# Attention over 4096 tokens on one core: TensorE's order goes by two key blocks, and it sums six key blocks of a chunk instead of five

## What is computed

```python
qkv = jnp.einsum('bnc,ce->bne', x, W_qkv)      # N = 4096 tokens, C = 128
q, k, v = jnp.split(qkv, 3, axis=-1)           # 4 heads of 32
q = l2norm_axis1(q)                            # over the tokens
k = l2norm_axis1(k)
sim = jnp.einsum('bihd,bjhd->bhij', q, k) * 10.0
attn = jax.nn.softmax(sim, axis=-1)
out = jnp.einsum('bhij,bjhd->bhid', attn, v)
```

## Time and profile before

| | us |
|---|---|
| runs of the kernel | 5823.16, 5830.10, 5831.83; median 5830.1 |
| profiled execution | 5824.59 |
| its span | 5822.9 |
| TensorE busy | 4673.1 (80%) |
| VectorE busy | 5061.3 (87%) |
| ScalarE busy | 3766.6 (65%) |
| GpSimd busy | 1666.2 (29%) |
| granted TensorE clock, mean | 0.944 |

### The profile page before, as it was taken

One profiled execution on the slowest core, in us unless ns is written; L12 is line 12 of the kernel. 1 busy time (PEld: TensorE's weight loads), 2 busy tenths in 40 slices (PEclk: granted clock), 3 DMA queues, 4 the chain that ended last, 5 costly groups with the idle time before them and its releaser, 6 DMA issues. The chain is left out here.

```text
span 5822.9 us, 99803 instructions
## 1 busy us (share of the span) xinstructions
PE 4673.1 (80%) x33816; PEld 1945.2 (33%) x33880; DVE 5061.3 (87%) x6502; ACT 3766.6 (65%) x4929; POOL 1666.2 (29%) x1274
## 2 busy tenths in 40 slices
PE   5677779998766777999876677799987667779997
PEld 2222433333322243333432224333343222433334
DVE  6799769998789977999868996799986899679998
ACT  3666459993466646999346663689934666369992
POOL 1488600000048860000005885000000588500000
PEclk9899989999889998999988999899998899989998
DMA  1000020000000002000000000200000000020000
GB/s 39 0 1 0 15 63 9 9 5 23 23 0 1 0 15 63 9 9 5 22 23 0 1 0 15 63 9 9 5 22 23 0 1 0 15 63 9 9 5 15
DMA packets 41642, 87.27 MB, mean 15 GB/s; under 512 B 11672, under 2 KB 27872, under 8 KB 38112
## 3 DMA queue, kind: packets, MB, share of 16 engines
q1 hardware_dynamic: 41184, 81.11, 5.2%
HBM read 26.55 MB, written 8.39 MB: 6 GB/s over the span
## 5 line engine op out<-in xcount | busy, mean ns | idle before, releaser
L1303 ACT ACTIVATE arena<-ps 128x1024 f32<-128x1024 f32 x2048 | 1915.2, 1035 | 194.4 <-PE ps L1266 177.6
L1332 DVE TENSOR_TENSOR arena<-arena 128x1024 f32<-128x1024 f32 x1664 | 1901.4, 1216 | 32.8 <-ACT arena L1303 32.3
L941 DVE TENSOR_TENSOR_SCAN arena<-ps,hlast,arena 128x512 f32<-128x512 f32 x1024 | 1259.1, 1265 | 5.2 <-DVE arena L923 3.2
L901 POOL TENSOR_TENSOR arena<-arena 128x1024 f32<-128x1024 f32 x512 | 1205.9, 2355 | 25.0 <-issue 1.8
L1266 PE MATMUL ps<-arena 128*32 128x512 f16 x16384 | 1095.0, 383 | 123.8 <-issue 62.3
L1249 PE MATMUL ps<-arena 128*32 128x512 f32 x8192 | 1070.0, 600 | 8.0 <-ACT arena L1303 4.3
L870 ACT ACTIVATE ps<-arena,amat 128x512 f32<-128x512 f32 x1024 | 691.9, 688 | 504.9 <-DVE arena L941 504.2
L838 PE MATMUL ps<-arena,ident 128*128 128x512 f32 x2048 | 980.8, 602 | 7.7 <-POOL arena L901 7.7
L1266 PEld LDWEIGHTS ps<-arena 128*32 128x32 f16 x16384 | 466.8, 97 | 980.2 <-issue 655.6
L1646 POOL MEMSET arena<- 128x1024 f32 x4 | 3.8, 956 | 2639.6 <-POOLq L101 2639.6
L923 DVE TENSOR_TENSOR arena<-arena,ps 128x1024 f32<-128x1024 f32 x512 | 610.8, 1193 | 53.1 <-remote 30.7
(11 more groups left out here) (246 smaller groups left out, 4401.5 us busy)
## 6 DMA issues: line engine op xcount, KB each, us to landing
arena<-x SPq DMA_DIRECT2D x32, 512.0 KB, 5.5
arena<-arena SPq DMA_DIRECT2D x64, 256.0 KB, 6.0
arena<-arena SPq DMA_DIRECT2D x64, 224.0 KB, 5.7
arena<-arena SPq DMA_DIRECT2D x28, 512.0 KB, 3.6
arena<-pe SPq DMA_DIRECT2D x256, 32.0 KB, 1.8
out<-arena SPq DMA_DIRECT2D x8, 1024.0 KB, 3.9
expw<-L_ffn_expert_w SPq DMA_DIRECT2D x1, 512.0 KB
wqkv<-L_attn_W_qkv SPq DMA_DIRECT2D x1, 192.0 KB
```

Of the source, the lines that this page charges most:

```text
L901: pool.tensor_tensor(halves(g[s % 4]), halves(hb[s % 4]), cs[s % 4].unsqueeze(1).broadcast_to([128, HD, CH]), ALU.mult).then_inc(hc_s, 1)
L941: dve.tensor_tensor_scan(halves(hb[s % 4])[:, h, :], da(s, h), halves(dbx[s % 2])[:, h, :], k.hlast[:, s, h, :], ALU.mult, ALU.add).then_i ...
L1303: act.activation(probs[p % 8], k.bank(2 * group[p], 2 * CH), ACT.Exp, scale=SCALE / SPLIT ** 2).then_inc(exp_s, 1)
L1332: dve.tensor_tensor(acc[p % 2], acc[p % 2], probs[p % 8], ALU.add).then_inc(acc_s, 1)
```

## The change

The summed blocks become every fifth block from 5 on: 5, 10, 15, 20, 25 and 30, so VectorE's additions go from 54 to 52 a chunk. TensorE's order becomes: scores of an even block and of the odd one after it, then the values of two blocks: after block j (odd, from 3 on) those of j-3 and j-2. The values of the last two blocks of a chunk, 30 (with its ones) and 31, come behind block 1 of the next chunk. The boundary steps move: `finish` from behind the scores of pair 4 to pair 5, the copy of the output from exponential 2 to 4, the division from addition 5 to 6. All waits keep their form.

```diff
--- before.py
+++ after.py
@@ -1218,7 +1218,7 @@
 
     group = [p % 3 for p in range(NPAIR - 1)] + [1]
 
-    direct = [j for j in range(NJ) if j % 6 == 5]
+    direct = list(range(5, NJ, 5))
     NA = NPAIR - 2 * len(direct)
 
     def first(c):
@@ -1268,15 +1268,14 @@
                                              start=True, stop=True, tile_position=(0, 32 * t))
                     last.then_inc(s_mm, 1)
 
-                    if p == 1 and not first(c):
-                        weigh(c - 1, NJ - 1)
-                    if p == 4 and not first(c):
+                    if p == 5 and not first(c):
                         finish(c - 1, 1 - q)
-                if j in (3, 4):
-                    weigh(c, 2 * j - 6)
-                    weigh(c, 2 * j - 5)
-                if j >= 5:
-                    weigh(c, j - 1)
+                if j == 1 and not first(c):
+                    weigh(c - 1, NJ - 2)
+                    weigh(c - 1, NJ - 1)
+                if j % 2 and j > 1:
+                    weigh(c, j - 3)
+                    weigh(c, j - 2)
 
         def staged(c, i, n):
             pe.wait_ge(staged_s[i], n * 16)
@@ -1287,6 +1286,7 @@
             staged(cc * 2 + 1, 1, cc + 1)
             staged(cc * 2 + 2, 0, cc + 1)
         staged(NCH - 1, 1, NCH // 2)
+        weigh(NCH - 1, NJ - 2)
         weigh(NCH - 1, NJ - 1)
         finish(NCH - 1, (NCH - 1) % 2)
 
@@ -1301,7 +1301,7 @@
                 act.wait_ge(pv_s, c * NJ + (p // 2 + 1))
                 act.wait_ge(acc_s, summed(c, p - 8))
                 act.activation(probs[p % 8], k.bank(2 * group[p], 2 * CH), ACT.Exp, scale=SCALE / SPLIT ** 2).then_inc(exp_s, 1)
-                if p == 2 and not first(c):
+                if p == 4 and not first(c):
                     keep_output(c - 1)
 
         act.sem_inc(exp_s, 3)
@@ -1330,7 +1330,7 @@
                 else:
                     dve.wait_ge(acc_s, summed(c, p) - 2)
                     dve.tensor_tensor(acc[p % 2], acc[p % 2], probs[p % 8], ALU.add).then_inc(acc_s, 1)
-                if p == 5 and not first(c):
+                if p == 6 and not first(c):
                     divide(c - 1)
 
         dve.sem_inc(pv_s, 4)
```

## The result

The changed kernel takes 6008.5 us (median of 4 runs, 5999.0 to 6012.5) against 5830.2: ratio 1.0306, interval 1.0288 to 1.0324. Forecast was 6001 us with 5950 to 6060. The profiled execution has a span of 6010.7 us, 187.8 more than before's 5822.9.

A forecast was written before the change was run, and what follows sets the result against it. A loop of TensorE and ScalarE over three score buffers was taken as the bound. Chunks 1 to 7 gain 5.7 us each, with chunk 0 and tail 44.1 a batch, +176 on 5824.6: 6001 us, range 5950 to 6060.

The forecast's parts named there:

- The bound: In the attention, a loop between TensorE and ScalarE over three score buffers fills a chunk, 65.3 us; VectorE runs just under.
- The values' wait: TensorE's value matmuls no longer wait for their exponentials; this removes only TensorE's idle time.
- Pairing: Two value blocks after four scores: each round takes 4.04 us for exponentials needing 3.68; 16 rounds are 64.6 us a chunk.
- Sixth block: Six summed blocks lie on the loop at 0.86 us each, 5.2 a chunk; VectorE's two additions fewer gain nothing.
- Joint and tail: Between chunks, scores 63 wait one exponential more, 0.92 us; at a batch's end the tail grows by 1.4 us.
- Steps: Moved boundary steps at a chunk's start: the final sum costs 0.27 us; ScalarE's copy and VectorE's division lie in slack.
- ScalarE's idle time: Sign: idle before the exponentials, waiting for scores, near 177.6 + 176 us or a little more.
- The total: Whole kernel: 5824.6 us of the profiled execution plus 176 us gives 6001 us, 3.0% slower; chance 85%.
- A: Rival, faster: VectorE bounds the attention, so two additions fewer a chunk give 73 us, 5752 us; chance 4%.
- B: Rival: rounds without ones are free as TensorE gets ahead; +0.8 us a chunk, about 5850 us; chance 4%.
- C: Rival: TensorE's granted clock falls to 0.97 in every chunk of the attention, 64 us more, 6065 us; chance 5%.

The follow-up runs named there:

- half-width values: Changed kernel with the value matmuls of every odd block over 256 of 512 queries, the other products left out: 5814.0 us, ratio 0.9982.
- five blocks and older values: Kernel before with values of block j-2 instead of j-1 behind the scores of block j, boundary steps moved, five summed blocks: 5777.4 us, ratio 0.9918.
- fastest kernel: Kernel before with values of block j-2, moved boundary steps, six summed blocks and their ones sums between the score pairs: 5726.3 us, ratio 0.9836.

## Why the prediction was right, and where not

- *The bound* (a loop of TensorE and ScalarE, not the busiest engine) held in both kernels, by the small additions. By the rule of the Trainium skill's page "Perfetto Trace Analysis", section Identifying the Most-Contended Engine, that the engine with the highest occupancy should be relieved first, VectorE's two additions fewer would have gained 73 us. The runs differ from it: with VectorE's additions over a quarter of their columns the time fell by 12 us in the kernel before and by none in the changed one. The sixth block gained only where TensorE's order had brought a chunk down to VectorE's own load. The Trainium skill's reading of a repeated gap, possibly too few buffers (it stands in the same page's section Optimization Strategy, not in the one that the prediction names), fits: the three score buffers give the loop its length. That more buffers would shorten it is not shown, as no run had a fourth: banks 0 to 5 hold the three, and 6 and 7 the output and the sums.
- *The values' wait* was called TensorE's idle time only. In the paired order that does no harm to the sum. In the old order it is not so: the wait starts the chain of 2.55 us that the prediction itself read at a summed block, and without it the break falls from 0.77 to 0.27.
- *Pairing*: rounds of 4.04 forecast, 4.04 measured. The half-width values show the mechanism at work: with 0.43 less in the gap the break is gone, by the 2.58 against 2.65 that the same steps give.
- *Sixth block*: 0.86 in full was forecast; the chunk shows 0.81 in the paired order. In the old order the prediction had 0.18 of each summed block hidden, against its own count of 0.77 + 0.11 for such a break; the run with six blocks shows nothing hidden (10.06 us for ten exponentials).
- *Joint and tail*: 4.96 forecast, 4.98 measured; +1.4 against +1.3.
- *Steps*: they were costed at 0.27 us a chunk lost to the final sum, in the paired order. The two rounds there came out as forecast (8.36). What they do in the old order, some 0.3 us a chunk gained, was not forecast; the expectation of that run had them free.
- *ScalarE's idle time* was forecast to grow by the whole 176 us; it grew by 158, and idle time of all kinds by 148.5 (194.4 to 342.9). Each break also costs the 0.11 between an exponential's length and its step, which the profile counts as busy: 8 more breaks in 32 chunks are 28 us, and 148.5 + 28 is the 176 again. That was in the sum but not in this check.
- *The total*: 6001 forecast, 6008.5 measured. The sum was added to the profiled execution, which lay 5.6 us under the median; the medians grew by 178 us and the attention by 175, against a forecast of 176. So it was the terms that met the time, and not errors that cancelled. One thing was left to luck: some chunks are about 1 us longer by the clock (last section), four before and one after.
- Rivals A and B fell (chunks of 71 us, and plain breaks of 0.27). C fell too: the granted clock stayed at 0.99 over the first batch's attention, as before, and at 1.00 past its first two chunks.

```profile
817.00:1391.00 574.00, 511.29 (x6572) 172.45 (x6568) 500.28 (x430) 486.73 (x519) 0.00 (x0) 0.99 0.05 12
959.00:1103.00 144.00, 127.71 (x1652) 43.14 (x1644) 125.90 (x108) 121.81 (x130) 0.00 (x0) 1.00 0.03 9
1103.00:1176.00 73.00, 64.08 (x828) 21.57 (x820) 64.25 (x56) 60.90 (x65) 0.00 (x0) 1.00 0.05 15
```

In the last two rows PE is busy for 128 of 144 us and 64 of 73, a share of 0.88 to 0.89 where it was 0.96 to 0.97, and stays at 2.4 GHz (columns as in the earlier trace rows). One argument against C was read from the first batch alone, that waits of 2.4 us leave the clock at 1.00; in later batches they did not always (last section).

## What to carry to other kernels

When two engines pass a few buffers round, add up one turn from start to start (the wait's release, the producer's work, whatever else is queued between, the hand-over) and compare it with the consumer's time for the buffers it holds; idle time on both and a busy third engine do not contradict a bound there. Work that is queued between two productions should be cut into pieces that fit the slack of one turn: here 0.86 us fits and 1.72 does not, so batching two and two, with a sixth sum, cost 3% (2.4% with five) and spreading the same work one by one, with older operands, gained 1.3% (1.6% with the sums split off too). Only then does moving work off the busiest engine pay: the sixth summed block cost the attention 23 us in one order and gained it 25 in the other. And the end of the stage has to be looked at by itself: there an engine that is off the path until then can be the one that is waited for (11.75 us of tail with five blocks and older values, 7.7 with six).

## What was not expected of the hardware

**The clock after a jump.** At the jump of TensorE's loop, twice a batch, the engine stands still for 2.1 to 2.4 us in the kernel before. At four of the eight jumps the granted clock stayed at 1.00, as at the one of the earlier trace rows. At the other four it was partly at 1.2 GHz just after, though the engine had worked up to the stop in both cases and the stops were of the same length (2.23 to 2.37 us, and 2.11 to 2.44 where it stayed). The stretch behind the earlier trace rows, then one in the second batch with its start:

```profile
1149.00:1153.00 4.00, 3.52 (x52) 1.41 (x56) 2.05 (x3) 2.74 (x4) 0.00 (x0) 1.00 0.08 28
2463.00:2467.00 4.00, 4.00 (x44) 1.47 (x36) 1.39 (x2) 2.11 (x3) 0.00 (x0) 0.58 0.02 5
```

```profile
2462.62 1.61 PE L1266 MATMUL ps<-arena 128*32 128x512 f16 x16 [2.23 <-issue]
```

It takes 1.61 us for the 16 matmuls that take 1.05 in the earlier trace rows. The chunk that follows such a jump is 65.7 to 66.2 us, where the others in its place are 64.8: 0.9 to 1.4 us each time, some 5 us in the whole kernel. In the changed kernel the stops are 1.5 to 2.0 us long, and the clock fell after one of the eight (0.57 in the 4 us from 5664; that chunk took 72.1 and not 71.0). In the fastest kernel they are 2.3 to 2.8 us, and it fell after one:

```profile
1128.88 0.61 PE L1272 MATMUL ps<-arena 128*32 128x512 f16 x8 [2.48 <-issue]
```

```profile
1129.00:1133.00 4.00, 4.00 (x36) 1.18 (x32) 1.87 (x3) 2.05 (x2) 0.00 (x0) 0.62 0.02 6
```

What decides at which jump the clock falls is not shown.

**The other stages.** Stages with the same code took different times: the span less the attention, up to the end of its divisions, is 3678.8 us before, 3691.6 after, 3671.9 with the steps alone, and 3694.5 with older values and five summed blocks. Each of these is one execution, and executions of one kernel differ as much: 5820.5 to 5835.5 us for the kernel before on one chip, and 5766.9 to 5789.2 for the one with older values and five blocks, whose profiled execution was the longest, at a mean clock of 0.939 where the shortest had 0.944. So it is not shown that the kernel makes the difference. Differences under some 15 us between two of these kernels should be read from their chunks and tails, not from their total.
